# Row sums and maxima of an attention kernel: transposes on PE replaced by block reductions on DVE

## What is computed

```python
kv = concatenate([context, latents], axis=1)         # 4 x (1601 + 256) x 512
q, k = rms_norm(latents @ Wq), rms_norm(kv @ Wk)     # 32 query heads, 8 key heads, 128 wide
v = kv @ Wv
scores = einsum('bhgqd,bhkd->bhgqk', qg, k) / sqrt(128)
probs = softmax(scores, axis=-1)
out = einsum('bhgqk,bhkd->bhgqd', probs, v) @ Wo
```

## Time and profile before

| | us |
|---|---|
| median of three runs | 2815.78 (2813.55 to 2817.94) |
| the profiled execution | 2816.99 |
| its span, first to last instruction | 2815.2 |
| PE busy | 2720.3 (97%) |
| POOL busy | 2377.3 (84%) |
| DVE busy | 2221.7 (79%) |
| ACT busy | 2029.4 (72%) |
| mean granted clock of PE, share of full speed | 0.986 |

### The profile page before, as it was taken

One profiled execution on the slowest core, in us unless ns is written; L12 is line 12 of the kernel. 1 busy time (PEld: TensorE's weight loads), 2 busy tenths in 40 slices (PEclk: granted clock), 3 DMA queues, 4 the chain that ended last, 5 costly groups with the idle time before them and its releaser, 6 DMA issues.

```text
span 2815.2 us, 47816 instructions
## 1 busy us (share of the span) xinstructions
PE 2720.3 (97%) x14812; PEld 2220.4 (79%) x14812; DVE 2221.7 (79%) x3596; ACT 2029.4 (72%) x3945; POOL 2377.3 (84%) x2320
## 2 busy tenths in 40 slices
PE   7899999999999999999999999999999999999974
PEld 5777878777878888888888888888888888888853
DVE  5577888888778878888778887787778888788873
ACT  3577777777767777777777777777777777777771
POOL 4399999898888888878889988888898888888893
PEclk9999999999999999999999999999999999999996
DMA  6756565565555454555545455554455445344310
GB/s 234 253 184 216 193 221 193 195 213 184 183 178 200 160 177 169 182 177 196 178 147 193 167 189 174 179 184 165 156 173 173 154 158 180 124 165 150 117 42 26
DMA packets 159434, 485.64 MB, mean 173 GB/s; under 512 B 16839, under 2 KB 27849, under 8 KB 159182
## 3 DMA queue, kind: packets, MB, share of 16 engines
q1 hardware_dynamic: 157592, 481.01, 50.5%
q10 hardware_dynamic: 1590, 1.58, 0.2%
HBM read 403.09 MB, written 79.43 MB: 171 GB/s over the span
## 4 chain that ended last, share of the span: by engine, by line
PE 79%; POOL 9%; issue 6%; DVE 4%; ACT 2%; DMA 1%; SPq 0%; POOLq 0%; ACTq 0%; DVEq 0%
PE K_ps L971 9%; PE K_ps L973 9%; PE K_ps L972 9%; PE OT_ps L1001 7%; PE S_ps L971 6%; PE S_ps L973 6%; PE S_ps L972 6%; POOL acc L906 5%; PE OT_ps L971 5%; PE OT_ps L972 4%; PE OT_ps L973 4%; POOL P_lo L888 2%; PE F_ps L971 2%; PE F_ps L972 2%; PE F_ps L973 2%
## 5 line engine op out<-in xcount | busy, mean ns | idle before, releaser
L906 POOL TENSOR_TENSOR acc<-acc,scores 128x512 f32<-128x512 f32 (+1 forms) x832 | 1120.8, 1347 | 40.4 <-ACT scores L1323 10.1
L888 POOL TENSOR_TENSOR P_lo<-scores,P_hi 128x512 fp32r<-128x512 f32 x672 | 898.4, 1337 | 211.3 <-ACT scores L1323 210.3
L1652 DVE SCALAR_TENSOR_TENSOR running_max<-S_ps,rk,running_max 128x512 f32<-128x512 f32 (+1 forms) x896 | 669.0, 747 | 250.2 <-ACT scores L1309 247.8
L1636 DVE TENSOR_TENSOR scores<-scores,Mb_ps 128x512 f32<-128x512 f32 (+1 forms) x960 | 648.7, 676 | 134.4 <-PE Mb_ps L1127 134.3
L1309 ACT ACTIVATE scores<-S_ps,rk 128x512 f32<-128x512 f32 (+1 forms) x960 | 651.6, 679 | 139.8 <-PE S_ps L973 120.1
L1323 ACT ACTIVATE scores<-scores 128x512 f32<-128x512 f32 (+1 forms) x960 | 596.9, 622 | 59.2 <-DVE scores L1636 57.1
L1322 ACT ACTIVATE P_hi<-scores 128x512 fp32r<-128x512 f32 x672 | 423.1, 630 | 293.7 <-DVE scores L1636 213.9
L971 PE MATMUL S_ps<-QT_hi,KT_hi 128*128 128x512 f32 (+1 forms) x960 | 496.9, 518 | 14.8 <-DVE running_max L1652 13.0
L971 PE MATMUL K_ps<-Wkv_hi,kvT 128*128 128x256 f32 (+1 forms) x1664 | 470.9, 283 | 2.4 <-DVE kvT L1709 2.4
L973 PE MATMUL K_ps<-Wkv_hi,kvT 128*128 128x256 f32 (+1 forms) x1664 | 471.1, 283 | 0.0
L972 PE MATMUL K_ps<-Wkv_lo,kvT 128*128 128x256 f32 (+1 forms) x1664 | 470.3, 283 | 0.0
(11 more groups left out here) (226 smaller groups left out, 4666.8 us busy)
## 6 DMA issues: line engine op xcount, KB each, us to landing
kvT<-kvT_scratch SPq DMA_DIRECT2D x403, 512.0 KB, 3.7
Wq_hi<-weight_halves_scratch SPq DMA_DIRECT2D x48, 512.0 KB, 5.4
Wq_lo<-weight_halves_scratch SPq DMA_DIRECT2D x48, 512.0 KB, 6.6
Wo_hi<-weight_halves_scratch SPq DMA_DIRECT2D x48, 512.0 KB, 4.7
Wo_lo<-weight_halves_scratch SPq DMA_DIRECT2D x48, 512.0 KB, 5.6
kvT_scratch<-built SPq DMA_DIRECT2D x45, 512.0 KB, 4.3
rinv_spread<-rinv_scratch SPq DMA_DIRECT2D x64, 256.0 KB, 4.8
Wkv_hi<-weight_halves_scratch SPq DMA_DIRECT2D x24, 512.0 KB, 5.6
```

The costliest lines, as they stand in the source:

```text
L888: e.tensor_tensor(P_lo[n % PB][0:r, :], prob(t)[0:r, :], f(P_hi[n % PB][0:r, :]), ALU.subtract)\
L906: e.tensor_tensor(a[0:r, :], a[0:r, :], prob(t)[0:r, :], ALU.add).then_inc(s_acc, 1)
L1636: e.tensor_tensor(d, d, Mb_ps[0:r, :], ALU.add).then_inc(s_d, 1)
L1652: e.scalar_tensor_tensor(a, src, k, a, ALU.mult, ALU.max).then_inc(s_top, 1)
```

## The change

- **Maximum.** DVE reduces `running_max` with a transposing reduction (`block_max`): each block of 32x32 is transposed and then reduced, so that element (32i+a, j) of the result, 128x16, is the maximum over the 32 partitions of group i in column 32j+a. PE transposes this 128x16 tile once (`turn_max`, one step later than before); DVE reduces over the four groups into 16x32 `nm`, and multiplies it with a piece of the identity into `spread`, 16x16x32, which holds row j only at place j. One product with a column of ones (`spread_max`, fp32r) then fills `Mb_ps`. DVE empties `MT` in the same step as PE's transpose, as its last job, no longer a step later.
- **Sums.** Three tiles of each half (`SUMMED`) are no longer added by POOL; DVE sums each by the same kind of reduction (`sum_tile`), one step after the exponential, and sums `acc` so too (`sum_blocks`). The up to four results are added up, and one fp32 product with `same` (1 where two rows have the same place in their group of 32) adds the four groups and turns the result to 16x32 (`add_blocks`). The reciprocal goes straight from this bank to `rrow`; the job `RT` is gone. `divide` follows `AT` at 6 steps, which is two steps earlier than before.
- **The last unit**, both halves (`LATE`): DVE sums all 15 tiles, POOL adds none.
- **`FULL`** has two tiles fewer in every batch (7, 5, 3, 3 become 5, 3, 1, 1): these are split into `P_hi` and `P_lo`. `EVENTS` takes its steps from `LIGHT`.
- `acc` and `built` have one buffer in place of two.

```diff
-    FULL = [[2, 3, 6, 7, 10, 11, 14], [4, 5, 10, 11, 14], [6, 7, 14], [6, 7, 14]]
+    FULL = [[4, 5, 10, 11, 14], [6, 7, 14], [14], [14]]
+    SUMMED = [[0, 7, 13], [0, 7, 12], [0, 5, 10], [0, 5, 10]]
+    LIGHT = [[2, 7, 11], [2, 7, 12], [], []]
...
+    SUMMED = [SUMMED[v // KVH] for v in range(UNITS - 1)] + [list(range(NJ))]
+    ADDED = [NJ * p + j for p in range(HALVES) for j in range(2, NJ) if j not in SUMMED[p // 2]]
+    LATE = [p for p in range(HALVES) if len(SUMMED[p // 2]) == NJ]
...
-            5: [("X", b + 1, turn(2 * h)), ("MT", 2 * v - 2)],
+            5: [("X", b + 1, turn(2 * h))],
+            6: [("MT", 2 * v - 2)],
...
-            12: [("RT", 2 * v - 3)],
...
-            20: [("MT", 2 * v - 1)],
-            21: [("O", 2 * v - 3, 0)],
+            21: [("MT", 2 * v - 1), ("O", 2 * v - 3, 0)],
...
-            27: [("RT", 2 * v - 2), ("QT", v, 1)],
+            27: [("QT", v, 1)],
...
     def divided(s):
-        return [x[1] for x in fill(s - 6) if x[0] == "RT"]
+        return [x[1] for x in fill(s - 6) if x[0] == "AT"]
...
             def turn_max(p):
-                e.wait_ge(s_top, NJ * (p + 1))
+                e.wait_ge(s_bm, p + 1)
                 out = take(("MT", p))
-                for i in range(4):
-                    ins = e.transpose(out[:, i * P:(i + 1) * P], top[:, i * P:(i + 1) * P], ident[:])
-                ins.then_inc(s_ff, 1)
+                e.transpose(out[0:16, 0:P], tops[:], ident[:]).then_inc(s_ff, 1)
...
-                for i in range(4):
-                    ins = e.transpose(Mb_ps[:, i * P:(i + 1) * P], nm[:, p % 2, i:i + 1].to_broadcast([P, P]), ident[:])
-                ins.then_inc(s_mb, 1)
...
+                e.matmul(Mb_ps[:], one[:].to_broadcast([16, P]), spread[:].rearrange("j i a -> j (i a)"), start=True, stop=True)\
+                    .then_inc(s_mb, 1)
+
+            def add_blocks(p):
+                if p == 0:
+                    e.wait_ge(s_same, 1)
+                e.wait_ge(s_bt, p + 1)
                 out = take(("AT", p))
-                for i in range(4):
-                    ins = e.transpose(out[:, i * P:(i + 1) * P], acc[p % 2][:, i * P:(i + 1) * P], ident[:])
-                ins.then_inc(s_ff, 1)
...
+                e.matmul(out[0:16, 0:32], sums[:, p % 2, :], same[:], start=True, stop=True).then_inc(s_ff, 1)
...
+            def block_max(p):
+                e.wait_ge(s_top, NJ * (p + 1))
+                if p:
+
+                    e.wait_ge(s_ff, F_AT["MT", p - 1] + 1)
+                e.tensor_reduce(tops[:], top[:].rearrange("p (j a) -> p j a", a=32), AX.X, ALU.max, apply_transpose=True)\
+                    .then_inc(s_bm, 1)
+
+            def sum_tile(t):
+                p, j = divmod(t, NJ)
+                e.wait_ge(s_p, t + 1)
+                e.tensor_reduce(blocks_of(p)[:, SUMMED[p // 2].index(j), :], prob(t).rearrange("p (j a) -> p j a", a=32), AX.X,
+                                ALU.add, apply_transpose=True).then_inc(s_bs, 1)
...
+                if 0 <= s - WAIT - 1 < NS and summed_tile(s - WAIT - 1):
+                    sum_tile(s - WAIT - 1)
+                for x in fill(s + 1):
+                    if x[0] == "AT":
+                        sum_blocks(x[1])
```

More of the change, by code:

```diff
@@ L227, in layer @@
         p, j = divmod(s - WAIT, NJ)
-        if j in FULL[p // 2] and j - 1 not in FULL[p // 2] and j < NJ - 1:
+        if j in LIGHT[p // 2]:
             EVENTS.append(s)
@@ L352, in layer @@
         top = sb("running_max", [P, QW])
-        acc = [sb(f"acc{i}", [P, QW]) for i in range(2)]
+        acc = sb("acc", [P, QW])
         OT_n = sb("OT_n", [P, QW])
@@ L400, in layer @@
         xrow = sb("xrow", [P, E])
[L401 removed]
+        built = sb("built", [P, 2, C, P], F32R)
         ident = sb("ident", [P, P])
         qkw = sb("qkw", [P, 3])
[L404 to L407 removed]
+        tops = sb("block_maxima", [P, 16])
+        nm = sb("negated_maxima", [16, 32])
+        spread = sb("maxima_on_diagonal", [16, 16, 32], F32R)
+        one = sb("one", [16, 1], F32R)
+        blocks = sb("block_sums", [P, 2, max(map(len, SUMMED[:-1])) + 1, 16])
+        sums = sb("block_totals", [P, 2, 16])
+        same = sb("same_in_block", [P, 32])
+        rrow = sb("rrow", [16, 32])
         rb_all = sb("rinv_spread", [P, QW])
@@ L1827, in _ @@
                 for x in fill(s - 1):
[L1828 removed]
+                    if x[0] not in ("KV", "Q", "MT"):
                         drain(x)
```

138 lines of the change are left out of this document (87 added, 51 removed).

## The result

The changed kernel took 2846.25 us (median of 4 runs, 2845.56 to 2850.80), the kernel before 2816.73 in the same session: a ratio of 1.0111, 95% interval 1.0095 to 1.0127. It is 30 us slower where 71 us faster was forecast (2745, range 2702 to 2790): direction and range were both missed. The forecast is 101 us short of what was measured.

The account below looks back on a forecast made before the run. PE's own work was taken as the bound until about 2690 us, POOL in the last 70. From 2817.0, -80 (PE), -22 (last unit) and +31 (waits) gave 2746, as median 2745 us; range 2702 to 2790.

Parts of the forecast that it names:

- PE's own work: PE's instructions outside the last unit: 59 us saved on maximum, sums and reciprocals, 21 us on `FULL`, together 80 us.
- last unit: Both last halves: with DVE summing all tiles, 70.7 us become about 51; 22 us saved, bounds 10 and 28.
- PE's waits: PE waiting for DVE's late maximum: 1.0 us per unit over 31 units, +31 us, bounds 0 and 62.
- the term of the small products: PE's saving per half on maximum, sums and reciprocals' transpose: 0.95 us, 59 us over 62 halves.
- The turned maximum: PE, each half: four transposes become one, 0.43 - 0.11 = 0.32 us saved.
- the reciprocals' transpose: PE, each half: this transpose goes, 0.11 us saved.
- The spread: PE, each half: four instructions become one split-type product of 512 columns, 0.43 - 0.23 = 0.20 us saved.
- The sums: PE, each half: four instructions become one fp32 product of 32 columns, taken at 0.11 us; 0.32 us saved.
- the step "where it will not fit": Steps 13 to 18 of a unit: block sum and earlier division make DVE's maximum late for PE, 1.0 us per unit.
- the price of the transposing reductions: DVE: 342 transposing reductions at 0.68 us each, 234 us, with 1.37 us each as upper end.
- Rival (b): DVE becomes the bound in the halves before the last unit: 74 us in place of 31, total 2780 us; chance 0.18.
- theory B: From the experiments, not the prediction: DVE has too much to do per unit, wherever the division stands; no chance given.

Follow-up runs that it names:

- experiment 4: Changed kernel with `FULL` and the self attention's places as before and no tile sums outside the last unit: 2798.94 us, ratio 0.9939 to the kernel before.
- (3): Changed kernel with `FULL` as before and, outside the last unit, one tile sum a half on DVE: 2826.35 us; or none: 2822.18 us.
- (8): Most of POOL's work on the weights' low parts left out for units 2 to 7: changed kernel 2808.41 us, kernel before 2803.54 us.
- 1: Changed kernel with only the division put back to step 18: 2841.06 us, ratio 1.0086 to the kernel before.
- the second run of 6: Changed kernel with `FULL`, the self attention's places and the division (step 18) as before, three tile sums a half kept: 2813.35 us, ratio 0.9990.
- the first and third of 7: First: changed kernel, self attention's places as before, 2839.22 us. Third: fastest version, last two batches with `FULL` lacking 6, 7 and DVE summing 5, 10, 2794.89 us.
- experiment 5: Changed kernel, no tile sums outside last unit, both tables as before: division at 18, 2802.78 us; old maximum, division at 18, 2792.75 us, at 16, 2803.93 us.

## Why the prediction was wrong

The sum's terms, as forecast and as the traces have them (2815.2 the old span):

| term | forecast | found |
|---|---|---|
| PE's own work | -80 | -42 |
| last unit | -22 | -18 |
| PE's waits | +31 | +92 |
| span | 2744 | 2847 (measured 2844.9) |

**PE's saving: the term of the small products failed.** The turned maximum saved its 0.32 us a half (in experiment 4 steps 5 and 20, from which the four transposes are gone, are 0.32 to 0.52 shorter; the single one, a step later, takes 0.11), the reciprocals' transpose its 0.11, and `FULL` its 0.17 a tile. The spread was to go from 0.43 to 0.23 and went to 0.62; before, the four transposes with their neighbours took 0.44. The sums were to go from 0.43 to 0.11. After, from the starts:

```profile
1515.57 0.28 PE L1001 MATMUL K_ps<-Wkv_hi,kvT 128*128 128x256 f32 x1
1515.78 0.23 PE L1162 MATMUL F_ps<-same_in_block,block_totals 128*16 128x32 f32 x2
1515.94 0.50 PE L999 MATMUL OT_ps<-P_hi,V_hi 128*128 128x512 f32 x1
1516.28 0.39 PE L1000 MATMUL OT_ps<-P_lo,V_hi 128*128 128x512 f32 x1
```

These are 0.21, 0.16 and 0.34 where 0.12 and 0.23 are usual without it: 0.36 in all. So a half saved 0.32 - 0.18 + 0.08 + 0.11 = 0.33 in place of 0.95 (21 us for 59), and with `FULL`'s 21 us it is 42. The prediction took the price of a product from rows in which like follows like; what it costs to change from one form to another was in none of its terms.

**PE's waits: the step "where it will not fit" had the right spot and the wrong law.** It named steps 16 to 18, the block sum and the division moved there, and gave 1.0 us a unit everywhere. I took for each of PE's products what its distance to the next start exceeds the usual one of the same neighbours: 45 us in the four stretches before, 137 after, by batch 25, 9, 2, 9 and 73, 32, 5, 27. The 92 us more are concentrated (48 and 23 in the first two batches, 18 in the fourth), not spread. In the third batch, from whose rows the 1.0 us a unit was worked out, PE waited 3 us more in all instead of 8: there the division runs in 1.18 us at step 16, where it had 1.66 at 18. The prediction used the division's 1.66 and 1.19 as a spread of durations instead of asking what stood beside them on POOL, so it could not see that 2.4 us splits, which exist only up to the second unit of the second batch, would land there. It also wrote that POOL's places matter and then gave them no price, and `LIGHT` it passed over altogether: the two tables, one costed as a pure gain of 21 us and one at nothing, are worth 44 us.

The splits explain why the change lost to the kernel before; they do not explain the whole distance to the forecast. Of its 101 us, 38 are PE's own work, 4 the last unit and 61 the waits (the rounded terms add up to 2 too many). Shorter splits give 38 back. What is left of the waits lies mostly in the second batch, where the places of the self attention account for 21 us in the kernel without tile sums (experiment 4), and in the fourth, where it stays open.

**Right:** the price of the transposing reductions; PE as the bound in the third batch; the last unit, in direction and nearly in size (77 us from the last scores on against 95, of it 15 to 18 from the part itself, where 22 was forecast); that the tile sums need room on DVE, at 4 to 11 us. **Rival (b)**, DVE becomes the bound, is refuted in its form: with 130 us less on DVE the time hardly moved (3), with the same instructions and shorter neighbours on POOL it fell by 38 (8). The experiments' theory B is not gone altogether: its numbers came in 1, in the second run of 6 and in the first and third of 7. In these DVE's instructions are late at some places, but their amount doesn't say where or by how much. A rival for this result would have been: long operations of POOL fall beside the division and the norm products. The division became 13 us longer in all over units 2 to 9, and the 14 norm products of the first batch took 2.2 us in the mean instead of 1.3, another 12.

The fastest version found keeps the sum of `acc` by blocks and the last unit and leaves tables, maximum and division as before: 2792.75 us, ratio 0.9919 (0.9904 to 0.9934), 24 us under the kernel before. Open remains how the gain of `FULL`'s tiles in the later batches and that of the maximum could be kept together; other places for the splits were not tried.

## What to carry to other kernels

When an operation's duration varies in the trace, find what runs beside it on the other engine before taking a mean: moving it by two steps can double it (2.75 against 0.68 us in unit 7 of experiment 5), and moving the neighbour can as well. Price a table of places step by step like any code, since here two such lines outweighed all the arithmetic that was saved. And price a small product among large ones by the starts of its neighbours on both sides, not by its own duration.
